# A gated attention and expert block on one core: the two chosen experts of a batch stored as five full chunks and one half chunk

## The reference, cut to what matters

```python
def _L0_ffn_ref(x, gate_W, W1, b1, W2, b2):      # D_MODEL 512, D_FF 352, 6 experts, TOP_K 2
    gate_logits = jnp.einsum('bd,ed->be', x.mean(axis=1), gate_W)
    gate_probs = jax.nn.softmax(gate_logits, axis=-1)
    topk_vals, topk_idx = jax.lax.top_k(gate_probs, TOP_K)
    topk_vals = topk_vals / topk_vals.sum(axis=-1, keepdims=True)
    ...
    h = jnp.einsum('bsd,bkdf->bksf', x, W1g) + b1g[:, :, None, :]
    h = jax.nn.gelu(h, approximate=False)
    eo = jnp.einsum('bksf,bkfd->bksd', h, W2g) + b2g[:, :, None, :]
    return jnp.einsum('bk,bksd->bsd', topk_vals, eo)
```

## Time and profile before

| | |
|---|---|
| profiled execution | 292.63 us |
| its span in the trace | 290.8 us |
| runs | 292.88, 293.05, 293.68 us |
| PE busy | 280.8 us, 97% |
| VectorE busy | 205.3 us, 71% |
| ACT busy | 108.8 us, 37% |
| GpSimd busy | 70.5 us, 24% |
| granted clock of PE | 0.998 of full |

### The profile page before, as it was taken

One profiled execution on the slowest core, in us unless ns is written; L12 is line 12 of the kernel. 1 busy time (PEld: TensorE's weight loads), 2 busy tenths in 40 slices (PEclk: granted clock), 3 DMA queues, 4 the chain that ended last, 5 costly groups with the idle time before them and its releaser, 6 DMA issues.

```text
span 290.8 us, 4400 instructions
## 1 busy us (share of the span) xinstructions
PE 280.8 (97%) x1426; PEld 227.6 (78%) x1426; DVE 205.3 (71%) x449; ACT 108.8 (37%) x191; POOL 70.5 (24%) x108
## 2 busy tenths in 40 slices
PE   6969999999999999989999999999999999999995
PEld 6858888888888888868786878878788777878874
DVE  7889887888788896888769455685474953846133
ACT  4744323223222225625343454337243272441010
POOL 4555345544554554422240000000000000000000
PEclk9999999999999999999999999999999999999999
DMA  6870123223262322279114019530576106630003
GB/s 218 274 235 1 37 73 108 76 81 101 76 197 95 108 72 75 72 216 289 40 72 145 2 43 339 177 132 0 157 242 240 50 2 212 196 136 1 0 0 144
DMA packets 21489, 34.44 MB, mean 118 GB/s; under 512 B 1864, under 2 KB 10062, under 8 KB 21468
## 3 DMA queue, kind: packets, MB, share of 16 engines
q1 hardware_dynamic: 18400, 24.16, 25.7%
q0 software_dynamic: 3040, 9.98, 10.5%
q10 hardware_dynamic: 28, 0.02, 0.0%
HBM read 24.97 MB, written 9.19 MB: 117 GB/s over the span
## 4 chain that ended last, share of the span: by engine, by line
PE 88%; DVE 7%; POOL 2%; issue 1%; ACT 1%; ACTq 0%; POOLq 0%; DVEq 0%
PE bank L1006 33%; PE bank L980 15%; PE bank L981 14%; PE bank L982 14%; PE bank L997 3%; PE bank L988 3%; PE bank L1122 2%; POOL x_ring L426 1%; PE bank L946 1%; PE bank L1058 1%; DVE x_odd L740 1%; DVE w_lo L720 1%; PE bank L1131 1%; DVE ctx_lo L733 1%; DVE hT_lo L613 0%
## 5 line engine op out<-in xcount | busy, mean ns | idle before, releaser
L980 PE MATMUL bank<-w_lo,ctx_hi 128*128 128x512 f32 (+1 forms) x96 | 38.0, 395 | 0.4 <-DVE ctx_lo L733 0.4
L981 PE MATMUL bank<-w_hi,ctx_hi 128*128 128x512 f32 (+1 forms) x96 | 37.5, 391 | 0.0
L982 PE MATMUL bank<-w_hi,ctx_lo 128*128 128x512 f32 (+1 forms) x96 | 37.4, 390 | 0.0
L720 DVE TENSOR_TENSOR w_lo<-w_raw,w_hi 128x512 fp32r<-128x512 f32 (+2 forms) x24 | 27.7, 1175 | 2.1 <-ACT w_hi L884 2.0
L980 PE MATMUL bank<-ctx_lo,w_hi 128*128 128x512 f32 (+1 forms) x72 | 28.6, 397 | 0.0
L981 PE MATMUL bank<-ctx_hi,w_hi 128*128 128x512 f32 (+1 forms) x72 | 28.2, 392 | 0.0
L982 PE MATMUL bank<-ctx_hi,w_lo 128*128 128x512 f32 (+1 forms) x72 | 28.1, 391 | 0.0
L732 DVE TENSOR_SCALAR ctx_hi<-act,mix 128x512 fp32r<-128x512 f32 x16 | 7.8, 486 | 28.6 <-ACT act L892 28.6
L892 ACT ACTIVATE act<-bank,b1T 128x512 f32<-128x512 f32 x16 | 10.9, 688 | 43.8 <-PE bank L982 42.5
L814 ACT ACTIVATE aT_hi<-bank 128x512 fp32r<-128x512 f32 x18 | 10.8, 598 | 40.9 <-PE bank L997 38.9
L819 ACT ACTIVATE a<-bank 128x512 f32<-128x512 f32 x19 | 11.4, 600 | 36.8 <-PE bank L1006 36.8
(11 more groups left out here) (173 smaller groups left out, 559.2 us busy)
## 6 DMA issues: line engine op xcount, KB each, us to landing
raw_ctx<-in_ctx SPq DMA_DIRECT2D x4, 1024.0 KB, 7.9
w_raw<-in_L_ffn_W SPq DMA_DIRECT2D x8, 512.0 KB
w_raw<-in_L_ffn_W SPq DMA_DIRECT2D x8, 448.0 KB, 6.2
x_even<-x_scratch SPq DMA_DIRECT2D x8, 257.0 KB, 3.4
x_odd<-x_scratch SPq DMA_DIRECT2D x8, 257.0 KB, 2.9
w_raw<-in_L_ffn_W SPq DMA_DIRECT2D x8, 256.0 KB, 4.0
out<-x_even SPq DMA_DIRECT2D x8, 256.0 KB, 2.2
out<-x_odd SPq DMA_DIRECT2D x8, 256.0 KB, 2.1
```

The lines of the kernel that those rows point to most:

```text
L720: dve.tensor_tensor(part_of(w_lo[s], piece), part_of(w_raw[s], piece), part_of(w_hi[s], piece).bitcast(FP32), ALU.subtract).then_inc(lo_do ...
L980: pe.matmul(dst, s_hi, m_lo, start=first, stop=False)
L981: pe.matmul(dst, s_hi, m_hi, start=False, stop=False)
L982: return pe.matmul(dst, s_lo, m_hi, start=False, stop=last)
```

## The change

**Chunks.** The 704 features of a batch's two experts are stored anew. Slot 0 holds the first expert's 352 features and the first 32 of the second (3 full chunks: `MA` = 96 and `MB` = 32). Slot 1 holds the other 320 of the second: two full chunks and one of `LW` = 64. For that half chunk the high halves of w1 stand in columns 0 to 63 of a stationary block and the low halves in columns 64 to 127, so one pass gives both products with the high half of the input, in partitions 0 to 63 and 64 to 127 of the bank. A second pass, 64 columns wide, adds high by low. ACT copies the upper half of the bank out (`half_copied`), VectorE adds it to the lower half (`fold`), ACT applies gelu, and `weigh_last` puts the high half of the result in partitions 0 to 63 of `a2_hi` and the low half in partitions 64 to 127. The last 64 rows of w2 are loaded twice, so one output pass covers both; a second one takes `a2_lo` by the low half of w2 together with the biases b2, which `fill_bias` and six rows of `b2_rows` supply. The half chunk so has 8 hidden passes and 8 output passes. A batch has 68 and 68 in place of 72 and 72.

**What comes with it.** Loads: 17 DMAs per batch instead of 10, among them one of 32 w1 columns (512 pieces of 128 bytes) and six of single rows of 2 KB. The last gelu of slot 0 is two instructions (96 and 32 partitions) and `split_high(b, 1, 2)` has one more. `choose` ends with three operations instead of one, `spread_mix` on VectorE has five instead of one, `split_low` of slot 1 has two operations for its piece 1 and three for its piece 2, and slot 0's piece 1 is 1024 instead of 896 wide. At the start, GpSimd (POOL) makes masks (seven operations of one or two columns, three fills) in place of three fills, and PE turns seven small tables of b1 instead of three.

**The seam of the stages.** The mix of batch 0 is spread into bank `o_ps[0]`, and PE waits no longer for `mix_ready` ahead of the next transposes. The first block of `hidden(0, 0)` (three passes) stands ahead of the last product of stage one; `hid_ps` names its two banks in the other order. Piece 2 of slot 0 is split one tile earlier (`split_high`, `split_low` at `TILES - 1`). `scale_logits(0)` stands ahead of `a_low`.

The diff, cut to its core (left out: helper slices, the small tables, the masks, `weigh`):

```diff
         hT_ps, aT_ps, y_ps, z_ps = banks[0:4]
-        t_ps, hid_ps, o_ps = banks[0:2], banks[2:4], banks[4:8]
...
+        W1_REST_DMAS, W2_DMAS = (2, 1), (3, 9)
...
+                sp.dma_start(part_of(first, 0), w1_cols(one, 0, P)).then_inc(w1_here[0], 16)
+                sp.dma_start(rest_of(first, 0, P + MA), w1_cols(one, P, F2)).then_inc(w1_rest_here[0], 16)
+                sp.dma_start(rest_of(first, P + MA, REST), w1_cols(two, 0, MB)).then_inc(w1_rest_here[0], 16)
+                sp.dma_start(blocks[0], w2_blocks(one, 0)).then_inc(w2_here[0], 16)
+                sp.dma_start(first[0:MA, last], w2_rows(one, full, F2)).then_inc(w2_here[0], 16)
+                sp.dma_start(first[MA:P, last], w2_rows(two, 0, MB)).then_inc(w2_here[0], 16)
+                if b > 0:
+                    sp.wait_ge(lo_done[1], len(PARTS) * b)
+                sp.dma_start(part_of(second, 0), w1_cols(two, MB, MB + P)).then_inc(w1_here[1], 16)
+                sp.dma_start(rest_of(second, 0, P + LW), w1_cols(two, MB + P, F2)).then_inc(w1_rest_here[1], 16)
+                sp.dma_start(blocks[1], w2_blocks(two, MB)).then_inc(w2_here[1], 16)
+                for half in range(2):
+                    sp.dma_start(second[half * LW:(half + 1) * LW, last], w2_rows(two, F2 - LW, F2)).then_inc(w2_here[1], 16)
+                for e, rows in ((one, (64, 65, 96)), (two, (66, 67, 97))):
+                    for row in rows:
+                        sp.dma_start(b2_rows[row:row + 1, :], b2[bass.ds(e, 1), :]).then_inc(w2_here[1], 16)
...
-                dve.tensor_scalar(mix1[:, :], top[:, 0:2], tinv[:, 0:1], tg[0:1, 1:2],
-                                  ALU.mult, ALU.mult).then_inc(mix1_ready, 1)
+                run(dve.tensor_scalar(mix1[:, 0:2], top[:, 0:2], tinv[:, 0:1], tg[0:1, 1:2], ALU.mult, ALU.mult))
+                run(dve.tensor_copy(mix1[:, 2:4].bitcast(FP32R), mix1[:, 0:2]))
+                dve.tensor_tensor(mix1[:, 4:6], mix1[:, 0:2], mix1[:, 2:4], ALU.subtract).then_inc(mix1_ready, 1)
...
-                dve.tensor_copy(mix[:, bass.ds((b % 2) * 2, 2)], t_ps[1][:, 0:2]).then_inc(mix_ready, 1)
+                spread, at = mix_bank(b), (b % 2) * 3
+                dve.tensor_copy(mix[:, at:at + 2], spread[:, 0:2])
+                dve.tensor_copy(mix[0:MA, at + 2:at + 3], spread[0:MA, 0:1])
+                dve.tensor_copy(mix[MA:P, at + 2:at + 3], spread[MA:P, 1:2])
+                run(dve.tensor_tensor(bias_mix[LW:P, :], spread[LW:P, 2:6], bias_mask[LW:P, :], ALU.mult))
+                dve.tensor_reduce(bias_of[LW:P, b % 2:b % 2 + 1], bias_mix[LW:P, :], AX_X, ALU.add).then_inc(mix_ready, 1)
...
+                elif piece == 1:
+                    dve.tensor_tensor(rest_of(hi, P + LW, REST), rest_of(raw, P, P + LW), rest_of(hi, P, P + LW).bitcast(FP32),
+                                      ALU.subtract)
+                    dve.tensor_tensor(rest_of(lo, 0, P), rest_of(raw, 0, P), rest_of(hi, 0, P).bitcast(FP32),
+                                      ALU.subtract).then_inc(lo_done[s], 1)
+                else:
+                    last = slice(WN - D, WN)
+                    dve.tensor_tensor(lo[MA:P, last], b2_rows[MA:P, :], lo[MA:P, last].bitcast(FP32), ALU.subtract)
+                    dve.tensor_tensor(lo[0:LW, last], raw[0:LW, last], hi[0:LW, last].bitcast(FP32), ALU.subtract)
+                    dve.tensor_tensor(lo[:, W1N:WN - D], raw[:, W1N:WN - D], hi[:, W1N:WN - D].bitcast(FP32),
+                                      ALU.subtract).then_inc(lo_done[s], 1)
+            def fold(b):
+                dve.wait_ge(half_copied, b + 1)
+                bank = hid_ps[(2 * FC - 1) % 2]
+                dve.tensor_tensor(act[0:LW, 0, :], bank[0:LW, :], act[0:LW, 0, :], ALU.add).then_inc(folded, 1)
+            def fill_bias(b):
+                dve.tensor_scalar(a2_lo[LW:P, FC - 1, :].rearrange("p (t s) -> p t s", s=P),
+                                  ones[LW:P, :].unsqueeze(1).to_broadcast([P - LW, TT, P]),
+                                  bias_of[LW:P, b % 2:b % 2 + 1], None, ALU.mult)
+            def weigh_last(b):
+                dve.wait_ge(gelu_done, (2 * b + 2) * FC + 1)
+                w = mix[0:LW, (b % 2) * 3 + 1:(b % 2) * 3 + 2]
+                src = act_last[0:LW, :]
+                c = FC - 1
+                run(dve.tensor_scalar(a2_hi[0:LW, c, :], src, w, None, ALU.mult))
+                dve.tensor_scalar(a2_lo[0:LW, c, :], src, w, None, ALU.mult)
+                dve.scalar_tensor_tensor(a2_hi[LW:P, c, :], src, w, a2_hi[0:LW, c, :].bitcast(FP32),
+                                         ALU.mult, ALU.subtract).then_inc(a2_ready, 1)
...
-                a_low(j - 1)
                 if j == PREP + 3:
                     scale_logits(0)
+                a_low(j - 1)
...
+                if j == TILES - 1:
+                    split_low(0, 0, 2)
...
-                for c in range(FC):
+                for c in range(FC - 1):
                     weigh(b, 1, c)
+                fill_bias(b)
+                fold(b)
+                weigh_last(b)
...
+                elif s == 0:
+                    sc.wait_ge(hid_done, 2 * FC * b + k + 1)
+                    sc.activation(act_last[0:MA, :], hid_ps[k % 2][0:MA, :], ACT.Gelu, bias=b1_of(0, c, slice(0, MA), chosen[0]))
+                    sc.activation(act_last[MA:P, :], hid_ps[k % 2][MA:P, :], ACT.Gelu,
+                                  bias=b1_of(1, FC, slice(MA, P), chosen[1])).then_inc(gelu_done, 1)
+                else:
+                    sc.wait_ge(hid_done, 2 * FC * b + k + 1)
+                    wait_primed(sc, a2_ready, (2 * b + 1) * FC + 1)
+                    sc.activation(act[0:LW, 0, :], hid_ps[k % 2][LW:P, :], ACT.Copy).then_inc(half_copied, 1)
+                    sc.wait_ge(folded, b + 1)
+                    sc.activation(act_last[0:LW, :], act[0:LW, 0, :], ACT.Gelu,
+                                  bias=b1_of(1, c, slice(0, LW), chosen[1])).then_inc(gelu_done, 1)
...
+                if j == TILES - 1:
+                    split_high(0, 0, 2)
...
+            def hidden_block(b, s, c, k):
+                if c < 2 and k == 0:
+                    pe.wait_ge(lo_done[s], len(PARTS) * b + c + 1)
+                if c == 0:
+                    pe.wait_ge(h2T_lo_done, KD * b + k + 1)
+                col0 = k * P if c == 0 else KD * P + k * REST + (c - 1) * P
+                bank = hid_ps[(s * FC + c) % 2]
+                if s == 1 and c == FC - 1:
+                    h_hi, h_lo = h2T_of(b, k)
+                    both, high = w_hi[1][:, col0:col0 + P], w_hi[1][:, col0:col0 + LW]
+                    if k < KD - 1:
+                        pe.matmul(bank[:, :], both, h_hi, start=(k == 0), stop=False)
+                    last = pe.matmul(bank[0:LW, :], high, h_lo, start=False, stop=False)
+                    if k == KD - 1:
+                        last = pe.matmul(bank[:, :], both, h_hi, start=False, stop=True)
+                    return last
...
+                    for k in range(1 if b == 0 and k6 == 0 else 0, KD):
+                        last = hidden_block(b, s, c, k)
...
+                        if s == 1 and c == FC - 1:
+                            pe.matmul(o_ps[t][:, :], a2[0], w_hi[1][:, place], start=False, stop=False)
+                            last = pe.matmul(o_ps[t][:, :], a2[1], w_lo[1][:, place], start=False, stop=True)
...
-                if j == PREP + 5:
-                    pe.wait_ge(mix_ready, 1)
...
-                    pe.wait_ge(aT_lo_done, PREP + 4)
+                    pe.wait_ge(h2T_lo_done, 1)
                     spread_mix(0)
...
+            pe.wait_ge(a_ready, TILES)
+            hidden_block(0, 0, 0, 0)
             pe.wait_ge(aT_hi_done, TILES)
```

167 lines of the change are left out of this document (90 added, 77 removed).

## The result

The changed kernel takes 290.5 us (median of 4 runs, 288.67 to 291.38) against 293.0 us before; the estimated ratio is 0.9888, interval 0.9851 to 0.9926 (the quotient of the two medians, 0.9915, lies inside it). In a second series it took 289.99 us (6 runs, 289.28 to 291.23; ratio 0.9876, 0.9835 to 0.9916). It is faster, by about 1.1% or 3.1 us over all ten runs (median 290.28, that of 30 runs of the kernel before 293.34), and not by the 5.0 us of the forecast: the first median lies 0.3 us above the range, the second in it. The profiled execution took 291.38 us, with a span of 289.6 us (before 290.8).

The account below looks back on a forecast made before the run. TensorE, busy 97% of the span, was taken to bound the kernel. Terms 3.25 + 1.0 + 1.45 - 0.6 - 0.1 = 5.0 us off 292.63 gave 287.6, forecast left at 287.7 us, range 285.4 to 290.2.

Parts of the forecast that it names:

- Output, 3.25 us: Four output passes fewer per batch: 2.75 us in batches 0 to 2 plus 0.5 us at the kernel's end.
- The tail: End of batch 3, `finish`: first addition 0.23 us earlier, the four additions 0.26 us shorter, 0.5 us gained.
- Hidden, 1.0 us: Four hidden passes fewer per batch: most saving lost waiting for chunk 1's weighing; 0.8 to 1.6 us, taken as 1.0.
- The seam, 1.45 us: Four gaps on TensorE between the stages: 0.61 - 0.43 + 0.69 + 0.59 = 1.45 us gained.
- (a): Seam, at 130.34: TensorE's wait for the copy of the mix goes, 0.61 us gained.
- (c): Seam, 142.85 to 143.78: three passes of block 0 fill the wait for ACT's `hT_hi`, 0.69 us gained.
- (d): Seam, 154.61 to 155.43: `split_low(0, 0, 2)` one tile earlier removes the wait for `weigh(0, 0, 1)`, 0.59 us gained.
- (b): Seam: `choose` with two more chained steps on VectorE is 0.43 us longer, all of it reaching TensorE.
- The wider split, -0.6 us: VectorE's longer `split_low(b, 1, 2)` delays transposes in batches 1 and 2; bounds 0 and 1.0 us, taken as -0.6.
- the mix, -0.1: Batches 1 and 2: mix 0.4 us later at a spread with about as much to spare, -0.1 us.
- The start, 0: GpSimd's seven new operations before its tables are mostly covered by idle time and a dropped fill; bounds 0 and 1 us.
- Loads too late: Rival: slot 0's w2 cast 1.2 to 3.3 us later, stalling batch 1; 288.7 to 290.5 us, chance 0.18.

Follow-up runs that it names:

- the experiment: Changed kernel with the high product of each token tile in the last chunk issued twice, so 12 output passes again; 292.0 us, ratio 0.9947.
- the quiet profile: Second profile of the changed kernel, run again with no edit: 289.39 us, span 287.6; median of that series 289.99 us, ratio 0.9876.
- masks: Changed kernel with GpSimd's seven one-column mask operations behind the first gathers instead of ahead of its tables; 291.33 us, ratio 0.9942.
- low halves: Changed kernel with `ffn_h_low` for k = 0 and 1 ahead of the split of slot 1's w2; 291.01 us, ratio 0.9917.
- loads: Changed kernel with `output(b, 1)` in chunk order, slot 1's loads held until all of slot 0's have landed; 288.59 us, ratio 0.9846.
- split: Changed kernel with `output(b, 1)` in chunk order, slot 1's w2 subtraction moved behind slot 1's first weighing in batches 0 to 2; 287.27 us, ratio 0.9773.
- the kernel before with masks: Kernel before plus GpSimd's seven one-column operations at the start (results unused) and a semaphore for the part number; 293.32 us, ratio 1.0005.

## Why the prediction was right, and where its sizes were off

The order of things was right: faster, output passes paid for, hidden passes mostly lost, seam won, little taken back. Of the forecast 5.0 us 3.1 came by the medians, and 4.4 in the stretches that its terms name; the rest went in the start. That the second median lies in the range and the first just above it is partly luck: the errors of the terms partly cancel, and how late the clock rises in a run moves the time by more than the distance to the edge. The forecast was also taken off the profiled execution, 292.63 us, 0.7 us below the median of 293.34. By its own steps:

- **Output, 3.25 us.** Measured 2.50 + 0.16 = 2.66, by the experiment 3.0. Batches 0 to 2 are right but for the slower first pass. The tail is 0.16 and not 0.5, because the step looked at `finish` and stopped there. The four additions did shrink from 2.74 to 2.48 us, but the end comes 5.2 us after their first one starts in both kernels (285.56 to 290.8, 284.38 to 289.6): the four stores move 1.05 MB at some 375 GB/s, 2.8 us, and in both kernels they follow one another without a gap (first issued 1.18 us earlier, end 1.2 us earlier), so they set the pace. The traffic of the changed kernel from 284 to 291 us, by the view of DMA, in 40 slices of 0.175 us:

```profile
GB/s 0 0 0 0 0 0 0 0 0 0 0 386 374 374 375 386 374 374 398 386 339 410 386 363 386 386 281 12 0 0 0 0 0 0 0 0 0 0 0 0
```

- **Hidden, 1.0 us.** Measured 1.10 in `hidden(b, 1)`. The wait for VectorE, four times, with 0.65 us each where 0.6 was foretold, is there; TensorE goes on 0.15 us after the multiply, inside the bounds of 0.05 and 0.26. With the slow first pass behind it the net is 0.65.
- **The seam, 1.45 us.** Measured 1.71. (a), (c) and (d) give 2.03 alone; (b) costs 0.3 to 0.4 and not 0.43.
- **The wider split, -0.6 us, and the mix, -0.1.** Measured -1.11: 0.56 and 0.54 us in batches 1 and 2, the pessimistic end of the bounds. The three parts of the split take 2.52 us in the first profile (196.74 to 199.26) and not 1.75, and the transposes behind them wait. With the split moved away 0.4 us of it comes back in batch 2. The direction was right, the size half again as large.
- **The start, 0.** This term left out most: 0.66 us in the quiet profile, 3.0 us in the first. The mechanism that I had priced (GpSimd late with its tables by its masks) did not occur. The change's own part is 0.16 us: the fill beside `ident` ends 0.20 us later than the one that stood there before (2.49 and 2.29). The rest is TensorE's clock, which no term had: its late rise (0.5 us in the quiet profile, 1.4 in the first) and its fall in the first (1.5).
- **Not named.** `hidden(b, 0)` gained 0.22 us in three batches: 12 of its 36 passes were 96 columns wide and stood 0.230 us apart, those of 128 columns 0.227. That "a pass over 96 has the same distance" was right within 0.003 us.
- **Loads too late.** The rival's mechanism is real (the cast begins 0.8 to 1.9 us later after the first issue than before, by profile) and was mostly covered by slack, as weighed: 0 to 0.26 us in the changed kernel.

The half chunk's chain took what was forecast (timeline of VectorE, batch 3):

```profile
278.54 0.68 DVE L791 TENSOR_TENSOR act<-bank,act 64x512 f32<-64x512 f32 x1
...
281.12 0.75 DVE L806 SCALAR_TENSOR_TENSOR ctx_hi<-act_last,mix,ctx_hi 64x512 fp32r<-64x512 f32 x1
```

It ends at 281.87, 1.85 us ahead of the first pass that needs it (283.72). The steps are the ones that were priced (0.68 and 0.75 us are shown), and where they were made 2.5 us longer, TensorE waited.

What stays open: what decides when the clock rises in a run and whether it falls at 20 us, and whether the changed start makes a late rise likelier (three profiles of the old start rise at 6.10, 6.26 and 6.96 us, eleven of the changed one at 6.14 to 9.42; that is too few to say).

## What to carry to other kernels

When passes are taken off the bound engine, ask at once what stands behind them for an operand: here four of eight per batch only moved TensorE in front of a multiply of VectorE, and a mere reordering of the passes behind it (all tiles of one chunk, then the next) gave about as much again as the whole change (3.0 us by the medians). Follow the tail to its last byte: a faster last computation gains nothing that the stores can't take. And a fix for a late load or a long VectorE operation must be followed through the queue it is put in, since all four such moves here (masks, low halves, loads, split) did little but change who waits.

## What I had not expected of the hardware

**The clock at the start.** The same program's clock rises to the full level at different times in different runs (6.14 to 9.42 us in the eleven profiles of the changed kernel and its variants), while TensorE does the same warming transposes, and in two of these profiles it falls again to its lower level for some 3 us, from 19.7 and 20.2 us. The low mean clock of 6 of the 26 runs of the kernel before fits such a fall (no trace of them is kept); such a run is 2.1 us longer (295.4 and 293.3 us).

**Fills of GpSimd hold VectorE.** In the kernel before with masks GpSimd ran a fill of 128 x 512 from 6.14 to 6.66 us, and VectorE's two short casts beside it took 0.64 and 0.53 us, where they take 0.17 without it. GpSimd's timeline:

```profile
6.14 0.52 POOL L429 MEMSET act_last<- 128x512 f32 x1
```

and VectorE's in the same execution:

```profile
6.05 0.64 DVE L565 CAST rank<-rank_i 128x16 f32<-128x16 int32 x1
6.17 0.53 DVE L567 CAST pslot<-pslot_i 128x16 f32<-128x16 int32 x1
```

Both end with the fill (6.69, 6.70); the first starts 0.09 us ahead of it, while GpSimd's last mask operation (6.00 to 6.20) still runs. `ident` has the same form in both kernels: it starts at 1.68; before, GpSimd fills from 1.77 to 2.29 and it ends at 2.38; in the changed kernel GpSimd fills `b2_rows` from 1.97 to 2.49 and it ends at 2.57, 0.19 us later. The Trainium skill ("SBUF — State Buffer", section "Who interferes with whom") says that a copy, cast or tensor_scalar of VectorE in a two port mode and a GpSimd instruction lock each other out for a whole instruction, whoever comes first; by that rule the price of GpSimd's work is where its long fill falls, not how many small operations it has, and the traces agree.

**Held instructions.** The three parts of the wider split start 0.70 and 0.61 us apart (196.74, 197.44, 198.05), with lengths of 0.69 and 0.68: the second, whose output begins in another group of 32 partitions than the first's, begins only when the first is over, the third overlaps by 0.07. The first, whose output is in another group than that of the instruction ahead of it, begins 0.03 us after that one's end (196.71), where the split of the kernel before overlapped its own by 0.08 (159.10 and 159.18). That is what the Trainium skill ("VectorE: DVE Perf Modes", section "Two Vector instructions with no wait between them") states; two held parts cost some 0.1 us each, 0.2 us a split, and so most of the 0.4 us by which the term of the wider split was too small over two batches.
